# Two attention stages of a one-core decoder: causal mask added inside the row maximum, value products moved directly behind the scores

## Time and profile before

| engine | busy us | share of the span |
|---|---|---|
| TensorE matmul | 2545.3 | 89% |
| TensorE weight load | 1829.6 | 64% |
| VectorE | 1705.5 | 59% |
| ScalarE | 1260.0 | 44% |
| GpSimd | 855.4 | 30% |

### The profile page before, as it was taken

The page is one execution under the profiler, slowest core; times in us unless marked ns, Lnnn a source line. Parts: engine busy times, 40 slices in busy tenths (PEclk is TensorE's granted clock), DMA queues, the critical chain, the costliest instruction groups (busy, mean ns, idle before and its releaser), DMA issues. The chain is left out here.

```text
span 2875.1 us, 49084 instructions
## 1 busy us (share of the span) xinstructions
PE 2545.3 (89%) x16401; PEld 1829.6 (64%) x16401; DVE 1705.5 (59%) x4509; ACT 1260.0 (44%) x3451; POOL 855.4 (30%) x687
## 2 busy tenths in 40 slices
PE   4998998989799889599998998978969899869997
PEld 2665665766544356477776776757956567449996
DVE  7875986588766644344445557873336578434443
ACT  2333654256455323444443445743432388324342
POOL 4533440045431044122221225641110044132222
PEclk8999999999899899799999999978989999989998
DMA  9001000000300333200001002042130210531110
GB/s 319 14 1 51 14 2 19 1 16 1 83 11 1 60 94 113 96 1 1 1 1 47 18 1 75 1 161 76 38 93 1 58 44 5 191 118 49 54 51 26
DMA packets 155268, 144.06 MB, mean 50 GB/s; under 512 B 62024, under 2 KB 139982, under 8 KB 154640
## 3 DMA queue, kind: packets, MB, share of 16 engines
q1 hardware_dynamic: 142880, 112.17, 13.6%
q0 software_dynamic: 10560, 27.19, 2.8%
q10 hardware_dynamic: 1584, 1.57, 0.2%
HBM read 99.70 MB, written 43.02 MB: 50 GB/s over the span
## 5 line engine op out<-in xcount | busy, mean ns | idle before, releaser
L979 POOL TENSOR_TENSOR room<-room 128x1024 f32<-128x1024 f32 x144 | 273.8, 1902 | 410.7 <-DVE room L912 410.6
L1454 PE MATMUL l3f_out<-room,Y 128*128 x624 | 141.0, 379 | 0.0
L906 DVE TENSOR_REDUCE room<-room 128x8 f32<-128x1024 f32 (+1 forms) x144 | 140.3, 975 | 0.8 <-ACT room L1057 0.8
L979 POOL TENSOR_TENSOR room<-room,Y 128x1024 f32<-128x1024 f32 x32 | 60.7, 1896 | 232.6 <-DVE Y L912 232.6
L3626 DVE SCALAR_TENSOR_TENSOR room<-l1x_v,room 128x512 f32<-128x512 f32 x128 | 86.9, 685 | 67.9 <-ACT room L3772 67.7
L1454 PEld LDWEIGHTS l3f_out<-room,Y 128*128 128x128 f32 x624 | 115.6, 190 | 14.2
L3772 ACT ACTIVATE room<-l1x_u 128x512 f32<-128x512 f32 x128 | 76.1, 598 | 77.2 <-PE l1x_v L3441 76.8
L1055 ACT ACTIVATE room<-l2a_scores,Y 128x128 f32<-128x128 f32 x256 | 71.0, 379 | 75.3 <-DVE Y L898 75.2
L1055 ACT ACTIVATE room<-l1a_scores,room 128x128 f32<-128x128 f32 x256 | 71.4, 386 | 58.3 <-DVE room L898 58.3
L1055 ACT ACTIVATE room<-l0x_scores,room 128x128 f32<-128x128 f32 x256 | 70.5, 384 | 59.2 <-DVE room L898 59.2
L623 PE MATMUL l2a_proj<-room 128*128 128x256 f32 x384 | 93.9, 387 | 0.0
(11 more groups left out here) (879 smaller groups left out, 6924.2 us busy)
## 6 DMA issues: line engine op xcount, KB each, us to landing
sorted_rows<-head SPq DMA_DIRECT2D x1, 16640.0 KB, 57.6
room<-in_L_ffn_w SPq DMA_DIRECT2D x16, 1024.0 KB, 12.6
room<-in_L_ffn_W SPq DMA_DIRECT2D x16, 1024.0 KB, 12.6
room<-in_ctx SPq DMA_DIRECT2D x32, 256.0 KB, 3.4
Y<-sorted_rows SPq DMA_DIRECT2D x62, 130.0 KB, 2.1
room<-sorted_rows SPq DMA_DIRECT2D x39, 130.0 KB, 2.1
room<-results SPq DMA_DIRECT2D x8, 512.0 KB, 7.1
room<-in_L_ffn_routed_w SPq DMA_DIRECT2D x4, 512.0 KB
```

The lines of the kernel that those rows point to most:

```text
L906: dve.tensor_reduce(rsum[:, u % 2, 0:SUMMED], p[:, u % (TURN + 1), 0:SUMMED, :], AX.X, ALU.add)
L979: pool.tensor_tensor(p[:, u % (TURN + 1), :, :], p[:, u % (TURN + 1), :, :], rinv[:, u % (TURN + 1), :].unsqueeze(2).to_broadcast([P, HEAD ...
L1454: mm = pe.matmul(obank[n % 2][:, 0:D], hT[:, n % 2, f, :], chip.room[:, bass.ds(at + (SLOT // 2 + f * D), D)], start=(f == 0), stop=(f == ...
```

## The change

Three flags are set in `attention_block`. `added` (`l3x`, as before, and now `l2a`): no mask matmul; the first score product starts the bank, VectorE adds the float32 causal mask to the scores, writes the negated sum back to the bank and takes the row extreme in the same instruction, four instructions of 128x128 for each half; the exponentials read the bank with scale -1. `between` (`l2a` alone): VectorE empties its projection banks of section 0 between the two halves' maxima. `adjacent` (`l2a` and `l0x`): TensorE does `values(t - VALUES)` directly behind `score(t)`, and ScalarE copies `out` directly behind the exponentials of half 0.

```diff
+    added = plan.mask == "timebias" or t_ in ("l2a",)
+    between = added and not small and not ctxsrc
+    adjacent = t_ in ("l2a", "l0x")
...
+                    mask = None if added else mask
                     if mask:
                         for a in range(2):
                             pe.matmul(banks[a][:, :].rearrange("p (i k) -> p i k", i=UNIT), chip.ident_b[:, :],
...
                 for t in range(T + VALUES + 2):
                     if t < T:
                         score(t)
+                    if adjacent and 0 <= t - VALUES < T:
+                        values(t - VALUES)
                     for x in at[(t, 0)]:
                         project(x)
                     if 0 <= t - TURN < T:
                         turn(t - TURN)
                     for x in at[(t, 1)]:
                         project(x)
-                    if 0 <= t - VALUES < T:
+                    if not adjacent and 0 <= t - VALUES < T:
                         values(t - VALUES)
...
+                def row_max(t, a):
...
+                    if added:
+                        addend = {"timebias": lambda: bias[:, b, :], "causal": lambda: chip.causal[:, :], "support": lambda: mask_b[:, g % 2, j, :]}[plan.mask]()
+                        for i in range(UNIT):
+                            op = dve.tensor_tensor_reduce(out=bank[:, i, :], in0=bank[:, i, :], in1=addend, scale=-1.0, scalar=FMAX, op0=ALU.add, op1=ALU.min,
+                                                          accum_out=nmx[:, t % 2, a * UNIT + i:a * UNIT + i + 1])
+                    else:
+                        op = dve.tensor_reduce(nmx[:, t % 2, a * UNIT:(a + 1) * UNIT], bank, AX.X, ALU.max, negate=True)
...
+                        row_max(t, 0)
+                        if between:
+                            for x in at[(t, 0)]:
+                                if not by_scalar(x[1]):
+                                    empty(x)
+                        row_max(t, 1)
...
-                sign = -1.0 if plan.mask == "timebias" else 1.0
+                sign = -1.0 if added else 1.0
...
+                def copy_out(u):
+                    b, st = divmod(u, S)
+                    act.wait_ge(pv_done, u + 1)
+                    act.copy(oT[:, b % 2, st * CS:(st + 1) * CS, :], out[:, 0:CS * P].rearrange("p (c q) -> p c q", c=CS)).then_inc(out_copied, 1)
+
                 for t in range(T + VALUES + 2):
                     if t < T:
                         exps(t, 0)
+                    if adjacent and 0 <= t - VALUES < T:
+                        copy_out(t - VALUES)
```

More of the change, by code:

```diff
@@ L506, in attention_block @@
         if plan.mask in ("keymask", "support"):
-            mask_b = sb("mask_b", [P, 2, PAIR, P], BF16)
+            mask_b = sb("mask_b", [P, 2, PAIR, P], F32 if added else BF16)
         if plan.mask == "timebias":
@@ L661, in score @@
                             wait_emptied(pe, (g, f))
-                        if plan.mask in ("keymask", "support"):
+                        if plan.mask in ("keymask", "support") and not added:
                             pe.wait_ge(mask_ready, g + 1)
@@ L885, in _ @@
                     biased(0)
+                def row_max(t, a):
+                    b = t // S
+                    g, j = divmod(b, PAIR)
+                    bank = scores[(2 * t + a) % 3][:, :].rearrange("p (i k) -> p i k", i=UNIT)
+                    dve.wait_ge(scores_ready, 2 * t + a + 1)
+                    if added:
[5 more added lines that the diff above has]
+                        op = dve.tensor_reduce(nmx[:, t % 2, a * UNIT:(a + 1) * UNIT], bank, AX.X, ALU.max, negate=True)
+                    if plan.mask == "support":
+                        dve.drain()
+                        op = dve.tensor_scalar(nmx[:, t % 2, a * UNIT:(a + 1) * UNIT], nmx[:, t % 2, a * UNIT:(a + 1) * UNIT], padcol[:, b:b + 1], None, ALU.min)
+                    op.then_inc(max_ready, 1)
@@ L887, in _ @@
                 for t in range(T + VALUES + 2):
                     if t < T:
[L889 to L902, removed]
@@ L916, in _ @@
                         for x in at[(t, sec)]:
-                            if not by_scalar(x[1]):
+                            if not by_scalar(x[1]) and not (between and sec == 0 and t < T):
                                 empty(x)
```

## The result

The changed kernel takes 2852.36 us (median of four runs, 2851.37 to 2855.11), the kernel before 2874.13 us beside it (2870.24 to 2874.85). The ratio is 0.992, with a 95% interval of 0.9909 to 0.9932: faster, clear of the 0.2% that a measurement tells. The forecast was 2857 with a range of 2847 to 2866.

The account below looks back on a forecast made before the run. TensorE's stream was taken to bound l2a, while in l0x TensorE and VectorE were both nearly full. Savings of 14.3 + 0 + 2.5 = 16.8 us from 2873.56 gave 2856.8, stated as 2857, range 2847 to 2866.

Parts of the forecast that it names:

- TensorE's stream sets `l2a`: In l2a TensorE is busy 324.5 of 329 us, so what leaves its stream leaves the time.
- The mask matmuls, 0.44 us a step: In l2a, without the mask matmuls, bank to scores goes from 2.36 to 1.92 us: 0.44 saved a step.
- The move in `l2a`, 0.07 a step: In l2a, moving the values from between projections makes bank to bank 1.73 instead of 1.82; 0.07 us a step taken.
- Scores to values 1.09: In l2a, values begin 1.09 us after scores; bounds about 0.12 less, at worst 1.51.
- The third rival: Direct passage from scores to values costs 0.42 us on top of 1.09; 7 us slower, 2880.7; chance 0.05.
- The second: Rival: direct passage from 64 rows to columns costs 0.17 us more over 57 steps; 7 us left, 2866.5; chance 0.14.
- the fourth: Rival: mask matmuls lie in time TensorE would spend anyway, so the change does nothing; 2873; chance 0.05.
- The first rival: Every shape change costs 0.17 us and each step with scores and values saves one; 23 us, 2850.5; chance 0.17.
- `l2a`'s cover: In l2a VectorE's 0.8 us more a step, 26 us in all, is covered; its results come in time.
- The last pair, 0 within 1.5: In l2a's last four steps and tail, without projections, gains and losses cancel: 0, with 1.5 us either way.
- `l0x`, 2.5 us: In l0x, 0.05 us over 32 steps (1.6) plus 1 us from the query bank's vanished wait: 2.5 us.
- one of the signs of being wrong: In l0x, TensorE waiting for copies of transposed probabilities would show the forecast wrong; slack was put at 0.25 us.

Follow-up runs that it names:

- experiment 1: Changed kernel with the value products back in their old place in l2a and l0x, mask still added in VectorE: 2871.08 us, ratio 0.9961.
- experiment 2: Changed kernel with l2a's old mask matmuls and old maximum, value products still moved in l2a and l0x: 2875.76 us, ratio 0.998.
- experiment 8: Changed kernel with two score and two value products alternating in l2a from step 3, nine shape changes a step: 2889.08 us, ratio 1.0053.
- experiment 5: Changed kernel with value products directly ahead of the step's scores, not behind them, in l2a and l0x: 2895.49 us, ratio 1.0073.
- experiment 6: Changed kernel with the value products moved behind the scores in all six attention stages: 2900.98 us, ratio 1.0085.

## Why the prediction was right, point by point

- **TensorE's stream sets `l2a`: right.** Up to step 28 the loop is 16.8 us shorter, as the block distances add up, and in 1226 to 1460 us there is still no wait of its matmuls. One reading in the forecast was off: its list before has "issue" in front of the values' weight loads of up to 0.8 us, not 0.4. Nothing in the sum hung on it.
- **The mask matmuls, 0.44 us a step: right** in the place where it is paid (1.92 and 12.1 us over 28 steps, measured in experiment 1). Alone it gave 10.3 over the loop, because the last pair's chain grew and the clock fell behind its waits.
- **The move in `l2a`, 0.07 a step: the term that was mis-sized.** It is 0.20: 0.09 at the bank in front of the old place, and 0.11 at the bank behind the values, which was slow (1.83 in place of 1.72). The forecast counted the distances around the values and took the distance from the bank behind them to the mask as a plain bank. In the earlier trace rows all three banks look alike at 1.82 or 1.83, since in the old order every bank has a change of shape on one side. Only 1.73, half of the sixteen records, showed the plain pace, and I used it once instead of twice. It cost the forecast 3 us: 4.9 measured up to step 28 (experiment 2) for 2.0 forecast.
- **Scores to values 1.09: right**, neither bound was touched. The third rival, slower by a dear direct passage, is out: 1.09 here and 0.175 a change in experiment 8. The second is out by the same 1.09, and the fourth by experiment 1.
- **The first rival was nearer in `l2a`**: a like price for each change of shape. It had 0.17, measured 0.175 (experiment 8) and 0.20 (`l2a`). Its sum was 23 us, mine 16.8, measured 21.8. It isn't the whole truth either: its price would give 4.8 us in `l0x` and 1 more for the wait, and the loop gave 3.7. The Trainium skill ("TensorEngine Tiling (Array Packing)", Key Properties) says that a changed tiling mode drains TensorE. These traces agree in that nearly every change costs time, but no row shows a drain as such, and the size differs with the block behind. It has no price for it; the prices here are from the rows.
- **`l2a`'s cover: right.** VectorE got 26 us busier, and in 1226 to 1460 us no matmul waited for it. Only in the last pair do the values wait 0.88 us for its copy.
- **The last pair, 0 within 1.5: right within that.** From the first to the last scores of the last pair it was 15.63 us (1497.38 to 1513.01) and is 14.67 (1471.50 to 1486.17): 1.0 us given.
- **`l0x`, 2.5 us: about right, by other terms.** The loop gives 3.7 and the stage's end takes 1 to 2 back, which the forecast didn't count. Of the four steps of a pair the one with the query bank gives 0.40 us, the others 0.15, 0.11 and 0.02; the forecast had 0.05 each and 0.18 for the wait. The copies were as near as forecast (0.25 us of slack): the weight loads of the values wait 2.3 us in six pieces in 284 to 395 us. That was one of the signs of being wrong, in small; TensorE's matmuls don't wait there. Experiments 5 and 6 show what lies behind that edge: 40 us in one, 17 in the other.
- **The number.** 2852.36 is at the lower edge of the forecast's own band (2852 to 2861) and near the first rival's 2850.5. Two terms in `l2a` were too small, the move by 3 us and the last pair by 1. The number held because both errors are small beside the mask's 12, not because every term was right.

## What to carry to other kernels

Count the changes of the array's shape in TensorE's stream, and price each on both sides: the block in front and the projection bank behind (a mask matmul behind showed almost nothing in `l0x`). Put the blocks of unlike narrow shapes next to each other where TensorE is the limit, but look first at when their inputs are ready; a block pulled ahead of its inputs costs a wait every round, and in `l0x` (experiment 5), `l1a` and `l2fa` that wait was many times what the changed shape gave. Waits of about 2 us mostly cost the clock behind them too (experiments 1 and 6). Look also at the stage's end, where no other work covers a wait. A mask added by an engine with time to spare is worth its matmul, less what the chain grows where no other work fills the stream.

## What the runs showed of the hardware that was not expected

`l2x` isn't touched by the change, yet its loop took 163.5 us before and 165.5 after. Two stretches of 20 us from its first scores on, before and after, columns as above. The granted clock is 1.00 in the first and 0.91 in the second, that is, full speed (2.4 GHz) throughout in the first and part of the time at the lower level (1.2 GHz) in the second.

```profile
1553.00:1573.00 20.00, 15.82 (x101) 11.30 (x100) 10.54 (x29) 8.69 (x25) 3.97 (x3) 1.00 0.07 21
```

```profile
1525.00:1545.00 20.00, 15.82 (x82) 11.35 (x83) 9.75 (x28) 8.71 (x25) 3.97 (x3) 0.91 0.08 21
```

The same sixteen matmuls, behind the same idle time of 3.6 us, took 3.69 us in the one trace and 5.38 in the other:

```profile
1558.55 3.69 PE L623 MATMUL l2x_proj<-room 128*128 128x256 f32 x16 [3.58 <-ACT room L1005]
```

```profile
1530.45 5.38 PE L626 MATMUL l2x_proj<-room 128*128 128x256 f32 x16 [3.59 <-ACT room L1020]
```

So TensorE, idle for the same 3.6 us, kept the clock in one trace and lost it in the other, and that cost 1.7 us. The nine further traces in which this stage is the same show 165.2 to 165.5 us there; the kernel before was the lucky one. In `l1a` the loop, where nothing is changed, follows the clock of its first 20 us: 153.8 us at 1.00 (before), 155.2 at 0.91 (after and four more), 156.3 to 156.8 at 0.83 (four traces). In `l0x` with the move it is 152.3 us at 1.00 (three traces), 153.3 to 153.7 at 0.91 to 0.94, 154.3 and 154.7 at 0.83; without the move 156.0 at 1.00, 157.0 at 0.94 and 157.4 at 0.91, 3.7 more at each level. Stage times that differ by 1.5 to 2 us say nothing before their clocks are compared.
